# Two graph attention layers over 32 graphs: P.V of a unit in one block, and guard and shares of all twelve heads in one step

## Chip, cores and metric

The kernel runs on one core of a Trainium2 chip. The metric is the device time of one execution in microseconds (us), as the median of several. The engines are TensorE (PE; PEld is its weight load), VectorE (DVE), ScalarE (ACT), GpSimd (POOL) and SyncE (SP), which here only issues DMAs.

## The reference, cut to what matters

There are 32 graphs of 256 nodes with 384 features, an adjacency matrix of 256 x 256 for each, and 12 heads of 32.

```python
h = relu(layernorm(x))
x = x + L0(h, adj, adj)      # bias = adj + adj
h = relu(layernorm(x))
x = x + L1(h, adj)           # bias = adj

# one layer
q, k, v = heads(h @ Wq.T), heads(h @ Wk.T), heads(h @ Wv.T + bv)
a = q @ k.T * 384 ** -0.5 + bias          # per head, 256 x 256
a = where(any(a != 0, row), a, -inf)
out = nan_to_num(softmax(a)) @ v
return out @ Wo.T + bo
```

All of it is float32. The projections are computed with each operand split in a high and a low part and three products of the parts.

## The kernel before

A *unit* is one layer of one graph, so there are 64 units. Each engine runs its own program of *slots*: slot k works on four units at once, `attend` = k, `project` = k + 1, `output` = k - 1 and `norm` = k + 2. What an engine does in a slot, and in which order, is a list written out by hand, one list for each engine (`slot` and, for TensorE, `stages`). Nothing reorders it: an instruction that waits holds up everything behind it on its engine. Layer 1 of a graph comes three units after its layer 0, so its statistics need the result of unit k - 3.

The steps of a unit:

- **Rows.** VectorE takes statistics (L485) and the mean (L491), GpSimd computes `inv_dev` (`invert_deviation`, L296 and L298), VectorE the `shift` (L497), ScalarE `normalise` (L417), TensorE turns the rows (`transpose_rows`, L694), ScalarE copies the high part (`rows_high`, L425), VectorE makes the low part (`rows_low`, L504).
- **Projections.** `project_queries` and `project_keys` (L714) fill a PSUM bank for each third c of the features, 0, 1 and 2. ScalarE's `qk_high` (L435) and VectorE's `qk_low` (L512) take it out into `split_qk`, and SyncE's `stack_quadrant` (L242) copies the parts into `stack`, three DMAs for each of four quadrants. Each quadrant serves three heads. `qk_high` 0 waits until all stack DMAs of the unit before have landed, since they read `split_qk`. `project_v` (L733) and `add_value_bias` (L520) give `values`.
- **Scores.** For each head (a *step*, 0 to 11), `scores` (L640) makes a 256 x 256 tile in one of two banks, `negate_scores` (L535) adds the bias, negates and takes each row's minimum, and `exps` (L389) the exponential with its row sums.
- **Turning.** P.V needs the probabilities turned. Heads 0 to 3 are turned in 32 x 32 blocks on VectorE (`turn_blocks`, L549) and the blocks moved by 16 DMAs (`move_blocks`, L232); heads 4 to 11 go through TensorE (`transposes`, L652) and ScalarE (`copy_probT`, L401).
- **Guard.** GpSimd folds each tile in three additions (`add_half`, L308; `add_rest`, L313 and L318), so that VectorE's `find_share` can tell a row of zeros. It takes the reciprocals of the sums (L557), the largest magnitude (L559) and their product, the share (L562), once for each group of four heads.
- **P.V and shares.** `weigh_values` multiplies group 1 in one part (L660) and groups 0 and 2 in another (L669, L660). The shares are spread (`spread_shares`, L410), turned (`transpose_shares`, L746), copied (L444) and multiplied with the heads (`scale_heads`, L572). GpSimd splits the result (`split_heads`, L327 and L330), and `project_out` (L758) and `result` (L581) finish the unit.

Query, key, row, value and output products share two PSUM banks in turn. A stage that takes a bank waits for the reader of its last content:

```python
MISC = {"rows": (0, 1), "qk": (0, 1, 0), "out": (1, 1), "v": (0, 1)}
```

So query block 2 can start only when `qk_low` 0 has read bank 0. SyncE's list in a slot was: stack quadrants 2 and 3 of `attend`, loads, moves 1, 3 and 0, stack quadrants 0 and 1 of `project`, move 2, store. A move of `attend` waits for all four `turn_blocks` and for P.V of the unit before.

## Time and profile before

| | |
|---|---|
| median of three runs | 1602.06 us (1599.18 to 1602.61) |
| profiled execution | 1602.71 us |
| its span, first to last instruction | 1600.8 us |
| TensorE, weight load | 97%, 88% busy |
| VectorE, ScalarE, GpSimd | 86%, 86%, 82% busy |
| DMA engines | 71% busy, 163 GB/s |
| granted TensorE clock | 0.997 of full |

A line of the profile names the kernel's line (L714), the engine, and the tiles as output<-input. "Idle before" is the time in which an engine stood still in front of an instruction, with what ended it. Ends of matmuls are modelled and overlap their followers, so on TensorE distances from start to start are what counts. A merged row of a timeline (x16) gives the first start and the length to the last end.

### The profile page before, as it was taken

What the parts mean: (1) busy time and instruction counts of PE and PEld (TensorE: products, weight loads), DVE (VectorE), ACT (ScalarE), POOL (GpSimd) and SP (SyncE); (2) the same over time, 40 slices, a digit from 0 to 9 for tenths busy, and PEclk for the clock granted to TensorE, in tenths of its full rate; (3) what the DMA queues carried; (4) which work ended last, traced back from release to release, by engine and by line L of the source; (5) the groups of instructions that cost most, each with busy time, mean ns of one, the idle gap of its engine ahead of it and who ended that gap; (6) DMA issues with size and microseconds to landing.
All of it is one profiled execution on the core that took longest, in us unless ns stands there. A gap on an engine that the chain in (4) does not pass through costs nothing.

```text
span 1600.8 us, 45924 instructions
## 1 busy us (share of the span) xinstructions
PE 1550.4 (97%) x13184; PEld 1402.1 (88%) x13184; DVE 1372.1 (86%) x5190; ACT 1368.9 (86%) x4297; POOL 1320.1 (82%) x1673
## 2 busy tenths in 40 slices
PE   5999999999999999999999999999999999999996
PEld 5888998889889889888898899898898899898895
DVE  5898888888888888888888888888888888888895
ACT  5888888888889888888888888888888888888885
POOL 3788888888888888888888888888888888888885
PEclk9999999999999999999999999999999999999999
DMA  8677777676677676776776776766767767767664
GB/s 246 133 158 158 164 168 175 147 173 155 159 177 168 152 177 150 163 176 148 167 160 157 175 169 157 172 155 154 180 156 164 158 162 164 176 153 171 153 137 113
DMA packets 132538, 260.22 MB, mean 163 GB/s; under 512 B 30400, under 2 KB 58560, under 8 KB 132288
## 3 DMA queue, kind: packets, MB, share of 16 engines
q1 hardware_dynamic: 132288, 257.28, 70.4%
q8 instruction: 108, 1.77, 0.5%
q14 instruction: 142, 1.16, 0.2%
HBM read 26.48 MB, written 12.58 MB: 24 GB/s over the span
## 4 chain that ended last, share of the span: by engine, by line
PE 71%; SPq 14%; DMA 8%; DVE 2%; issue 2%; ACT 2%; POOL 0%; POOLq 0%; ACTq 0%; DVEq 0%
PE misc_bank L714 19%; PE misc_bank L758 12%; PE probT_bank L652 10%; PE misc_bank L733 10%; PE score_bank L640 8%; DMA stack<-split_qk 8%; SPq L242 7%; SPq L232 6%; PE values_bank L660 6%; PE values_bank L669 2%; PE misc_bank L694 2%; PE values_bank L746 2%; DVE split_qk L512 1%; ACT split_qk L435 1%; ACT prob L389 1%
## 5 line engine op out<-in xcount | busy, mean ns | idle before, releaser
L389 ACT ACTIVATE prob<-neg,guard 128x256 f32<-128x256 f32 x1536 | 764.2, 510 | 2.8 <-DVE guard L535 2.7
L308 POOL TENSOR_TENSOR half<-neg 128x256 f32<-128x256 f32 x768 | 550.9, 738 | 35.5 <-DVE guard L535 8.1
L535 DVE CUSTOM_DVE_ANT_0 neg<-score_bank,bias 128x256 f32<-128x256 f32 x1536 | 568.7, 416 | 7.6 <-PE score_bank L640 6.6
L401 ACT ACTIVATE probT<-probT_bank 128x512 f32<-128x512 f32 x512 | 290.8, 597 | 71.3 <-PE probT_bank L652 71.1
L640 PE MATMUL score_bank<-stack 96*128 96x256 f32 x1536 | 316.4, 308 | 2.9 <-DMA stack<-split_qk 1.7
L389 ACT ACTIVATION_READ_ACCUMULATOR prob<-neg,guard 128x1 f32 x1536 | 309.2, 201 | 0.0
L652 PE MATMUL probT_bank<-identity,prob 128*128 128x128 f32 x2048 | 307.3, 273 | 1.0 <-ACT prob L389 0.7
L313 POOL TENSOR_TENSOR half<-half 128x512 f32<-128x512 f32 x192 | 247.1, 1287 | 15.1
L640 PEld LDWEIGHTS score_bank<-stack 96*128 96x128 f32 x1536 | 221.1, 191 | 30.5 <-DVE guard L535 26.1
L652 PEld LDWEIGHTS probT_bank<-identity,prob 128*128 128x128 f32 x2048 | 242.4, 141 | 5.9 <-ACT prob L389 1.1
L435 ACT ACTIVATE split_qk<-misc_bank 128x512 fp32r<-128x512 f32 x192 | 114.6, 597 | 105.7 <-DMA stack<-split_qk 80.4
L512 DVE TENSOR_TENSOR split_qk<-misc_bank,split_qk 128x512 fp32r<-128x512 f32 x192 | 131.6, 685 | 79.0 <-ACT split_qk L435 79.0
L549 DVE STREAM_TRANSPOSE blocks<-prob 128x256 f32<-128x256 f32 x512 | 188.9, 416 | 1.6 <-ACT prob L389 1.1
L327 POOL TENSOR_SCALAR headsT_high<-headsT 128x256 fp32r<-128x256 f32 (+1 forms) x128 | 66.2, 517 | 107.9 <-DVE headsT L572 102.7
L318 POOL TENSOR_TENSOR guard<-half 128x256 f32<-128x256 f32 x192 | 141.5, 737 | 15.1
L520 DVE TENSOR_TENSOR values<-misc_bank,v_bias 128x384 f32<-128x384 f32 x128 | 71.0, 555 | 86.0 <-PE misc_bank L733 86.0
L330 POOL TENSOR_TENSOR headsT_low<-headsT,headsT_high 128x256 fp32r<-128x256 f32 (+1 forms) x128 | 130.4, 1019 | 10.7
L660 PE MATMUL values_bank<-probT,values 128*32 128x256 f32 x2048 | 135.5, 382 | 0.0
L341 POOL TENSOR_TENSOR rows<-rows,o_bias 128x384 f32<-128x384 f32 x128 | 127.0, 1013 | 0.0
L535 DVE DVE_READ_ACCUMULATOR2_ANT guard<- 128x1 f32 x1536 | 125.8, 82 | 0.0
L714 PE MATMUL misc_bank<-rowsT_high,w_low_0q 128*128 128x256 f32 x288 | 88.0, 305 | 14.6 <-DVE split_qk L512 10.7
L660 PEld LDWEIGHTS values_bank<-probT,values 128*32 128x32 f32 x2048 | 59.9, 109 | 43.8 <-issue 10.8
(92 smaller groups left out, 3988.3 us busy)
## 6 DMA issues: line engine op xcount, KB each, us to landing
stack<-split_qk SPq DMA_DIRECT2D x768, 192.0 KB, 3.7
moved<-blocks SPq DMA_DIRECT2D x1024, 64.0 KB, 2.0
rows<-x SPq DMA_DIRECT2D x32, 384.0 KB, 5.2
out<-rows SPq DMA_DIRECT2D x32, 384.0 KB, 2.8
bias<-adj SPq DMA_DIRECT2D x32, 256.0 KB, 5.2
neg<-w0q SPq DMA_DIRECT2D x1, 576.0 KB, 4.4
prob<-w0k SPq DMA_DIRECT2D x1, 576.0 KB, 6.4
probT<-w0v SPq DMA_DIRECT2D x1, 576.0 KB, 7.4
```

The costliest lines, as they stand in the source:

```text
L308: nc.gpsimd.tensor_tensor(half[:, step % GROUP, :, :], n[:, :, 0:N // 2], n[:, :, N // 2:N], ALU.add).then_inc(half_done, 1)
L313: nc.gpsimd.tensor_tensor(half[:, :, :, 0:N // 4], half[:, :, :, 0:N // 4], half[:, :, :, N // 4:N // 2], ALU.add).then_inc(quarter_done, 1)
L389: nc.scalar.activation(prob[:, step % PROB, q, :], neg[:, step % NEG, q, :], ACT.Exp, scale=-1.0, bias=guard[step // GROUP][:, step % GROU ...
L401: nc.scalar.activation(probT[:, n % PROBT, :, :].rearrange("p a b -> p (a b)"), probT_bank[n % 2][:, :], ACT.Copy).then_inc(act_copy_done, 1)
L535: nc.vector.tensor_tensor_reduce(out=neg[:, step % NEG, q, :], in0=score_bank[step % 2][:, q * N:(q + 1) * N], in1=bias[u.t % GRAPHS][:, q ...
L549: turn = nc.vector.transpose(blocks[:, :, :, at:at + HEAD], of)
L640: mm = nc.tensor.matmul(score_bank[step % 2][:, q * N:(q + 1) * N], stack[:, g, 0, c * N + q * P:c * N + (q + 1) * P], stack[:, g, 1, c * ...
L652: mm = nc.tensor.transpose(probT_bank[n % 2][:, k * N + q * P:k * N + (q + 1) * P], prob[:, step % PROB, q, k * P:(k + 1) * P], identity[: ...
L660: mm = nc.tensor.matmul(into[a * HEAD:(a + 1) * HEAD, :], values[u.k % 2][:, k, h * HEAD:(h + 1) * HEAD], probT[:, (h - MOVED) % PROBT, k, ...
L714: mm = nc.tensor.matmul(into, w[:, k, cols], r[:, k, :], start=(k == 0 and n == 0), stop=(k == CH - 1 and n == 2))
L733: mm = nc.tensor.matmul(misc_bank[MISC["v"][i]][:, 0:H], r[:, k, where], w[:, k, :], start=(k == 0 and n == 0), stop=(k == CH - 1 and n == 2))
L758: mm = nc.tensor.matmul(misc_bank[MISC["out"][i]][:, 0:H], r[:, k, where], w[:, k, :], start=(k == 0 and n == 0), stop=(k == CH - 1 and n ...
```

## The change

P.V of a unit becomes one block of 48 matmuls in the slot after its scores, and the two parts of the heads are now groups 0 and 1 (512 wide) and then group 2 (256 wide). `guard` becomes one tile for all groups, and `find_share` works once on all twelve heads. Row minima get two places, for even and odd units. The bias ring has three tiles, and a bias is loaded one slot later. All five lists are rewritten: among others all four stack quadrants of a unit are issued in one slot, in turn with the moves. The number of instructions on TensorE stays. The diff, cut to its core:

```diff
-        guard = [sb(f"guard{i}", [P, GROUP, TILES, 1 + N // 8]) for i in range(GROUPS)]
-        sums = [sb(f"sums{i}", [P, HEADS, TILES]) for i in range(2)]
+        guard = sb("guard", [P, GROUPS, TILES, GROUP, N // 8 + 2])
+        sums = [sb(f"sums{i}", [P, GROUPS, TILES, GROUP]) for i in range(2)]
...
-        NEG, PROB, PROBT = 4, 4, 8
+        NEG, PROB, PROBT = 4, 4, TURNED
...
-            return slice(0, GROUPS, 2) if part else slice(1, 2)
+            return slice(2, 3) if part else slice(0, 2)
...
-                sync.wait_ge(heads_ready, u.before(1).count(PARTS, 2))
+                sync.wait_ge(heads_ready, u.before(1).count(PARTS, 1))
...
+                    (load_rows, norm, 0), (load_bias, project, 0), (move_blocks, attend, 3),
+                    (move_blocks, attend, 2), (stack_quadrant, project, 0), (move_blocks, attend, 0),
+                    (stack_quadrant, project, 1), (move_blocks, attend, 1), (stack_quadrant, project, 2),
+                    (stack_quadrant, project, 3), (store, output, 0),
...
-                pool.wait_ge(guard_done, u.before(1).count(2 * GROUPS, 2 * g + 2))
-                nc.gpsimd.tensor_tensor(guard[g][:, :, :, 1:], half[:, :, :, 0:N // 8], half[:, :, :, N // 8:N // 4],
+                pool.wait_ge(guard_done, u.before(1).count(2, 2))
+                nc.gpsimd.tensor_tensor(guard[:, g, :, :, 1:1 + N // 8].rearrange("p q h a -> p h q a"), half[:, :, :, 0:N // 8], half[:, :, :, N // 8:N // 4],
...
-                groups, heads = part_groups(part), headsT[:, 0:1 + part, :]
+                groups, heads = part_groups(part), headsT[:, 0:2 - part, :]
...
+                    (split_heads, output, 1), (add_half, attend, 5), (add_half, attend, 6), (add_half, attend, 7),
+                    (add_rest, attend, 1), (add_half, attend, 8), (add_half, attend, 9), (invert_deviation, norm, 0),
+                    (add_half, attend, 10), (add_half, attend, 11), (add_rest, attend, 2), (add_half, project, 0),
+                    (add_half, project, 1), (add_output_bias, project, 0), (add_half, project, 2),
+                    (add_half, project, 3), (add_rest, project, 0), (split_heads, attend, 0), (add_half, project, 4),
...
-                act.wait_ge(heads_ready, u.count(PARTS, 0 if n >= GROUP else -1))
+                act.wait_ge(heads_ready, u.before(1).count(PARTS, 1 if step < 2 * GROUP else 2))
...
-                act.wait_ge(shares_done, u.count(GROUPS, 3 if part else 2))
+                act.wait_ge(shares_done, u.count(1, 1))
...
+                    (copy_probT, output, 7), (normalise, project, 0), (normalise, project, 1),
+                    (copy_probT, output, 8), (rows_high, project, 0), (rows_high, project, 1), (exps, output, 11),
+                    (copy_probT, output, 9), (exps, attend, 0), (exps, attend, 1), (spread_shares, output, 0),
+                    (exps, attend, 2), (copy_probT, output, 10), (copy_probT, output, 11), (copy_sharesT, output, 0),
+                    (spread_shares, output, 1), (exps, attend, 3), (qk_high, project, 0), (exps, attend, 4),
+                    (qk_high, project, 1), (copy_sharesT, output, 1), (exps, attend, 5), (exps, attend, 6),
+                    (copy_probT, attend, 4), (qk_high, project, 2), (exps, attend, 7), (copy_probT, attend, 5),
+                    (exps, attend, 8), (exps, attend, 9), (exps, attend, 10), (copy_probT, attend, 6),
...
+            def find_share(u, _):
+                dve.wait_ge(exp_done, u.count(2 * HEADS, 2 * HEADS))
+                nc.vector.reciprocal(inverse[:, :, :, :], sums[u.k % 2][:, :, :, :]).then_inc(guard_done, 1)
+                dve.wait_ge(eighth_done, u.count(GROUPS, GROUPS))
+                at = u.k % 2
+                nc.vector.tensor_reduce(largest[:, :, :, :].rearrange("p g q h -> p (g q h)"),
+                                        guard[:, :, :, :, at:at + 1 + N // 8].rearrange("p g q h a -> p (g q h) a"),
+                                        AX.X, ALU.max, apply_absolute_value=True).then_inc(guard_done, 1)
+                dve.wait_ge(guard_done, u.count(2, 2))
+
+                dve.wait_ge(spread_done, u.before(1).count(PARTS, PARTS))
+                nc.vector.scalar_tensor_tensor(out=share[:, :, :, :],
+                                               in0=largest[:, :, :, :], scalar=0.0, in1=inverse[:, :, :, :],
                                                op0=ALU.not_equal, op1=ALU.mult).then_inc(shares_done, 1)
...
+                    (qk_low, project, 0), (negate_scores, attend, 6), (scale_heads, output, 1), (qk_low, project, 1),
+                    (negate_scores, attend, 7), (negate_scores, attend, 8), (qk_low, project, 2),
+                    (result, output, 0), (negate_scores, attend, 9), (statistics, norm, 0),
+                    (negate_scores, attend, 10), (mean, norm, 0), (result, output, 1), (statistics, norm, 1),
+                    (mean, norm, 1), (negate_scores, attend, 11), (shift_rows, norm, 0),
+                    (add_value_bias, project, 0), (add_value_bias, project, 1), (negate_scores, project, 0),
+                    (rows_low, norm, 0), (rows_low, norm, 1), (negate_scores, project, 1), (find_share, attend, 0),
+                    (negate_scores, project, 2), (turn_blocks, project, 0), (negate_scores, project, 3),
+                    (turn_blocks, project, 1), (turn_blocks, project, 2), (negate_scores, project, 4),
+                    (scale_heads, attend, 0), (turn_blocks, project, 3), (negate_scores, project, 5),
...
-            def weigh_turned(u, g, into):
+            def weigh(u, g, into):
                 for k in range(TILES):
+                    of_blocks = moved[:, :, k, :].rearrange("p a (h q i) -> p h q a i", h=MOVED, q=TILES)
                     for a in range(GROUP):
                         h = GROUP * g + a
+                        of = of_blocks[:, h, :, :, :] if h < MOVED else probT[:, h - MOVED, k, :]
                         mm = nc.tensor.matmul(into[a * HEAD:(a + 1) * HEAD, :],
-                                              values[u.k % 2][:, k, h * HEAD:(h + 1) * HEAD],
-                                              probT[:, (h - MOVED) % PROBT, k, :], start=(k == 0), stop=(k == TILES - 1))
+                                              values[u.k % 2][:, k, h * HEAD:(h + 1) * HEAD], of,
+                                              start=(k == 0), stop=(k == TILES - 1))
                 return mm
 
+            def weigh_values(u, _):
+                pe.wait_ge(values_done, u.count(TILES, TILES))
+                for moves in blocks_moved:
+                    pe.wait_ge(moves, u.count(16 * QUADS, 16 * QUADS))
+                pe.wait_ge(act_copy_done, u.count(TURNED, 2 * GROUP - MOVED))
+
+                pe.wait_ge(heads_done, u.before(1).count(PARTS, 1))
+                weigh(u, 0, values_bank[0][:, 0:N])
+                weigh(u, 1, values_bank[0][:, N:2 * N]).then_inc(heads_ready, 1)
+                pe.wait_ge(act_copy_done, u.count(TURNED, TURNED))
+
+                pe.wait_ge(sharesT_done, u.count(PARTS, 1))
+                weigh(u, 2, values_bank[1][:, 0:N]).then_inc(heads_ready, 1)
...
-                pe.wait_ge(heads_done, u.count(PARTS, 1) if part else u.before(1).count(PARTS, 2))
-                for g in range(1 + part):
+                if part == 0:
+                    pe.wait_ge(heads_done, u.before(1).count(PARTS, 2))
+                else:
+                    pe.wait_ge(sharesT_done, u.count(PARTS, 1))
...
+                    (transpose_rows, project, 0), (transpose_rows, project, 1), (transposes, output, 9),
+                    (scores, attend, 1), (transposes, output, 10), (scores, attend, 2),
+                    (project_queries, project, 0), (transposes, output, 11), (scores, attend, 3),
+                    (project_keys, project, 0), (project_queries, project, 1), (scores, attend, 4),
+                    (transpose_shares, output, 0), (weigh_values, output, 0), (scores, attend, 5),
+                    (project_keys, project, 1), (scores, attend, 6), (transpose_shares, output, 1),
+                    (scores, attend, 7), (transposes, attend, 4), (project_queries, project, 2), (scores, attend, 8),
+                    (project_keys, project, 2), (scores, attend, 9), (project_out, output, 0),
+                    (transposes, attend, 5), (transposes, attend, 6), (scores, attend, 10), (project_out, output, 1),
+                    (scores, attend, 11), (project_v, project, 0), (transposes, attend, 7), (project_v, project, 1),
+                    (transposes, attend, 8), (scores, project, 0),
```

A line of "..." marks what is left out; the lists, `find_share` and `weigh_values` as they were stand in the code above. Other lines of the diff follow from these: `BIASES` for `GRAPHS` in the bias's index, `minimum(u)` (0 for even units, 33 for odd) where the row minimum is written and read, `2 - part` for `1 + part` in the widths of the shares.

## Rows read from the trace of the kernel before

**Rows 1.** The page's part 1: busy us, share of the span, instructions.

```profile
PE 1550.4 (97%) x13184; PEld 1402.1 (88%) x13184; DVE 1372.1 (86%) x5190; ACT 1368.9 (86%) x4297; POOL 1320.1 (82%) x1673
```

**Rows 2.** Timeline, TensorE: start us, length; the transposes that open four slots.

```profile
49.96 0.60 PE L652 MATMUL probT_bank<-identity,prob 128*128 128x128 f32 x4
...
782.87 0.60 PE L652 MATMUL probT_bank<-identity,prob 128*128 128x128 f32 x4
...
806.82 0.60 PE L652 MATMUL probT_bank<-identity,prob 128*128 128x128 f32 x4
...
1536.78 0.60 PE L652 MATMUL probT_bank<-identity,prob 128*128 128x128 f32 x4
```

**Rows 3.** The waits: us in total, times, longest us.

```profile
POOL headsT_high L327 <- DVE headsT L572: 102.7, 63, 3.1
POOL var_eps L296 <- DVE mean_var L491: 81.2, 64, 18.7
ACT split_qk L435 <- DMA stack<-split_qk: 80.4, 47, 3.0
...
PEld misc_bank L714 <- DVE split_qk L512: 22.7, 34, 1.6
...
PEld misc_bank L714 <- DVE rowsT_low L504: 19.3, 64, 1.6
```

**Rows 4.** Timelines of TensorE, VectorE, SyncE, ScalarE, 799 to 828 us.

```profile
799.82 0.60 PE L652 MATMUL probT_bank<-identity,prob 128*128 128x128 f32 x4
...
802.97 0.68 DVE L512 TENSOR_TENSOR split_qk<-misc_bank,split_qk 128x512 fp32r<-128x512 f32 x1
...
803.68 4.47 SPq L242 DMA_DIRECT2D stack<-split_qk  x6
808.25 3.27 SPq L232 DMA_DIRECT2D moved<-blocks  x4
...
812.24 5.10 SPq L242 DMA_DIRECT2D stack<-split_qk  x6
819.27 7.53 SPq L232 DMA_DIRECT2D moved<-blocks  x12
...
820.33 0.60 ACT L435 ACTIVATE split_qk<-misc_bank 128x512 fp32r<-128x512 f32 x1 [1.51 <-DMA stack<-split_qk]
```

**Rows 5.** Timeline, TensorE: the P.V blocks of one slot and what follows.

```profile
783.40 1.07 PE L660 MATMUL values_bank<-probT,values 128*32 128x256 f32 x16
784.40 0.45 PE L733 MATMUL misc_bank<-w_high_0v,rowsT_low 128*128 128x384 f32 x1
784.68 0.34 PE L733 MATMUL misc_bank<-w_low_0v,rowsT_high 128*128 128x384 f32 x1
...
792.00 1.07 PE L669 MATMUL values_bank<-moved,values 128*32 128x256 f32 x16
792.89 1.05 PE L660 MATMUL values_bank<-probT,values 128*32 128x256 f32 x16
```

**Rows 6.** Timelines of VectorE, GpSimd, TensorE, 781 to 790 us.

```profile
781.48 0.56 DVE L581 TENSOR_TENSOR rows<-misc_bank,rows 128x384 f32<-128x384 f32 x1
...
783.92 1.99 POOL L341 TENSOR_TENSOR rows<-rows,o_bias 128x384 f32<-128x384 f32 x2
...
783.99 0.96 DVE L497 SCALAR_TENSOR_TENSOR shift<-mean_var,inv_dev 128x2 f32<-128x2 f32 x1
...
787.30 0.49 PE L694 MATMUL misc_bank<-identity,normed 128*128 128x128 f32 x3
...
789.22 0.35 PE L714 MATMUL misc_bank<-rowsT_high,w_low_1q 128*128 128x256 f32 x1
```

**Rows 7.** The groups of instructions: count, busy us, mean ns, idle before.

```profile
L389 ACT ACTIVATE prob<-neg,guard 128x256 f32<-128x256 f32 x1536 | 764.2, 510 | 2.8 <-DVE guard L535 2.7
...
L308 POOL TENSOR_TENSOR half<-neg 128x256 f32<-128x256 f32 x768 | 550.9, 738 | 35.5 <-DVE guard L535 8.1 <-POOL guard L318 0.4
...
L559 DVE TENSOR_REDUCE largest<-guard 128x8 f32<-128x264 f32 x192 | 72.1, 376 | 1.3 <-POOL guard L318 1.3
```

124 lines of the change are left out of this document (28 added, 96 removed).

## Prediction

> **What bounds the kernel now.** I read the busy table first [rows 1]: TensorE is busy 1550.4 of 1600.8 us and the others at most 86%. So the time is TensorE's order of work plus whatever it waits for. Then I measured the slot. Its marker is the transpose block `(transposes, output, 8)`, which opens each slot of the old order. It stands at 49.96 us in the first full slot and at 1536.78 in the last, 61 slots later, with one ordinary slot at 782.87 to 806.82 [rows 2]. That is 1486.8 / 61 = 24.37 us per slot on average against 23.95 in the ordinary one. Reading all the slots off the same rows, about 25 of 61 are 23.94 to 23.99 long, none is shorter, and the longest are 25.6. So there is a firm floor of 23.94 and an irregular 0.43 above it.
>
> The waits name both [rows 3]. The irregular part is the weight load of L714 (`project_queries`, c = 2) waiting for `split_qk` of L512: it needs bank 0 back from `qk_low` 0. Behind that stands ScalarE's L435 (`qk_high` 0), which waits 80.4 us in 47 places for the DMAs of `stack`. TensorE stands up to 1.6 us there at a time. The regular part is L714 (c = 0) waiting 64 times, some 0.3 us each, for `rows_low`.
>
> The DMA chain behind the irregular part: `qk_low` 2 ends at 803.65, SyncE issues six stack DMAs, four moves, one store, six stack DMAs, and the last lands at 820.33, when ScalarE's `qk_high` 0 starts [rows 4]. That is 16.7 us; the last six stacks take 8.1 of it, from the first issue at 812.24 to the landing. SyncE's issue is most of a slot's length: 12 moves in 7.53 us are 0.63 each, six stacks in 4.47 are 0.75 each, so 16 and 12 of them are 19.1 us, before loads and stores.
>
> **The change part by part.** I lay one new slot out from t = 0 at `(transpose_rows, project, 0)`, with the block lengths of the old slot. TensorE gets the same instructions in another order: three transposes are 0.33 us, four 0.36 to 0.44, a score step 0.24 to 0.32, nine query or key matmuls 1.07, nine value or output ones 1.58, sixteen of P.V 0.89. With 0.39 of waiting before query block 0 that puts query 0 at t = 2.4, query 1 at 5.2, P.V at 7.0, query 2 at 12.2, its keys from 13.6 to 14.7, `project_out` at 14.9 and 17.6, `project_v` at 19.4 and 21.4, the next slot at 23.7. ScalarE, by its own order and lengths, comes to `qk_high` 0 at 9.2, to 1 at 11.4, to 2 at 14.7.
>
> *P.V in one block.* Sixteen P.V matmuls that stand alone take 1.00 us to the next kind (783.40 to 784.40) and leave the first matmul behind them at 0.28 where its fellows take 0.175 to 0.18; sixteen that are followed by more of their kind take 0.89 (792.00 to 792.89) [rows 5]. So one block end costs 0.11 + 0.10. The entry costs about as much again (0.33 from a score step where 0.23 is usual, and a first step 0.02 longer): 0.12. One of two ends and entries goes: 0.33 us a slot. Changes between transposes and other matmuls number the same in both orders (nine each), so they cost nothing. The block now waits for all moves and, before its last sixteen at 8.8, for the last `copy_probT`, done at 7.4; score step 5 and the keys are queued behind it. The moves land some 4 us before it. Nothing is added. TensorE's own work: 23.94 - 0.31 (the wait at L714, c = 0) - 0.33 = 23.30.
>
> *The wait for `rows_low`.* In the old order 1.92 us pass from `transpose_rows` 1 to L714 (787.30 to 789.22) over 1.6 us of work [rows 6]; in the new one the work in between is 1.67 (transposes 9 and 10, scores 1 and 2). `rows_high` 1 no longer stands behind `copy_probT` 9 on ScalarE, but `copy_probT` 8 and both `rows_high` come in one run. I keep 0.30. This gives a floor of 23.60.
>
> *The chain that feeds it.* `result` 1 at 781.48, statistics, mean, GpSimd's `inv_dev`, and `shift`, which ends at 784.95: 3.47 us [rows 6]. The shift of two numbers takes 0.96: it starts at 783.99, 0.07 behind GpSimd's L341, and ends when the first L341 does. In the new order an `add_half` (L308, 738 ns [rows 7]) follows `inv_dev` in place of L341, and one mean fewer stands in the chain (0.13). Then `normed` 1 comes 4.7 us after `project_out` 1, and TensorE reaches `transpose_rows` 1 at 4.84: no wait. If the shift kept its 0.96, 0.15 us a slot would come on top, 9 us in all.
> The Trainium skill (SBUF — State Buffer, "Who interferes with whom") has this as a rule: a VectorE instruction with two SBUF inputs waits for the whole of a GpSimd instruction that reads SBUF. The trace's 0.96 agrees. By the rule the merged `find_share` meets it once where three met it, but behind a longer GpSimd instruction (L341); this changes no term.
>
> *Guard and shares in one step.* Two of three reciprocals, reductions and share instructions go from VectorE. The reduction has 792 elements: between 0.38 (one old one, L559, 264 elements [rows 7]) and 3 x 0.38 = 1.13; I take 0.95, nearer the upper row, since its length grows with the elements. It starts after the last exponentials of the unit, at t = 2.9 by my layout, and its shares are done at about 4.7. The next `negate_scores` (step 2) ends at 5.4, and score step 4 needs it at 6.3: covered by 0.9. If the cover went, each 0.1 would cost 6 us. GpSimd must have its last `add_rest` ready by 3.0; it is ready at 1.7. The heads are now multiplied first 512 wide, then 256: `project_out` 0 at t = 14.9 waits for a GpSimd step of 1.2 us after a VectorE step that ends at 12.8: 0.9 spare.
>
> *Bias ring of three, load moved.* The load waits for a unit three back, which is past; it is 1.0 us of SyncE's time either way, and the bias is needed 10 us later. Nothing.
>
> *SyncE's order and the stall.* This is the large term. `qk_low` 2 took 3.8 us from the end of the key matmuls of c = 2 (799.82 to 803.65 [rows 4]); now it takes 1.5, since ScalarE reaches `qk_high` 2 just as they end. Behind it come 3 stacks, 4 moves, 3 stacks, 4 moves, 6 stacks: four moves more than now, the store behind instead of in between. Three stacks cost 1.9 us while the queue is not full and 2.25 at the pace of six (4.47); four moves cost 2.5 at the free pace and 3.27 behind six stacks. So the last six start between 8.8 and 11.0 us after `qk_low` 2, where now 8.6, and land 8.1 later. The queue never holds more than three stacks before them, so I take the free pace with a little more, 9.1: a chain of 17.2, with ends at 16.7 and 19.1. `qk_low` 2 ends at t = 16.2, so the last stack lands at 16.2 + 17.2 - 23.6 = 9.8. Query block 2 stands at t = 12.2 and wants `qk_low` 0 (in VectorE's order at 11.0 to 11.6), so the DMA may land as late as 10.5. There are 0.7 us of spare where there is none now. The chain has scattered by about 2 us from slot to slot (slots 23.94 to 25.6), so some slots still wait: 0.15 on average, and I add 0.10 for small margins (0.1 to 0.5 us) at `result` 0, `value_bias` 1 and ScalarE's `qk_high` 1. New slot: 23.60 + 0.25 = 23.85.
>
> *Head and tail.* The head has the same loads and waits: 0. At the end all shares of the last unit hang on its last exponentials, and two GpSimd splits (L327 and L330, 512 wide 2.0 and 256 wide 1.2 us) follow each other where one did: +2.4 us.
>
> **Sum.** 62 x (24.37 - 23.85) = 32.2; less 2.4: 29.8. Span 1600.8 - 29.8 = 1571.0. The profiled run took 1602.7, 1.9 over its span, and the median of the runs is 0.65 below it: 1571.0 + 1.9 - 0.65 = 1572.
>
> **Rivals.**
> (a) *SyncE becomes the bound; slower.* The last stack's landing releases `qk_high` 0, and on ScalarE stand between it and `qk_high` 2: one exponential step and two more after `qk_high` 1 (three steps of two instructions of L389 at 510 ns [rows 7], pipelined to 0.98 a step: 2.9 us), two `qk_high`, a shares copy, a probability copy; with `qk_low` 2 it is 6.1 us. That closes a loop with the DMA chain. At 17.2 it is 23.3, under the floor. At the upper end, 19.1, it is 25.2, and the slot is that long: 62 x 0.83 + 2.4 = +54, 1656. It decides from a chain of 18.3 on. For it: SyncE issues for 20 of 24 us now. Against: the queue drains while it issues moves.
> (b) *No change.* GpSimd has 1320 us of work, 21.3 a slot, and now waits 184 us, 3.0 a slot, in two places [rows 1, 3]. The new order has it wait for three results of others (both heads, the mean) with 2.3 us to spare at 23.6. If these waits stay at 3.0, the slot stays at 24.3: 1600.
> (c) *The spread is absorbed too.* Slot 23.60: 62 x 0.77 - 2.4 = 45: 1557. It rests on the landings: the last of the six stacks now lands 3.0 us after SyncE has issued it (817.34 to 820.33 [rows 4]).
> By the Trainium skill (DMA: Bandwidth & Descriptors, "Anatomy of one DMA", a fit for another issuing path) 192 KB would take 2.4 us, so the chain would be 0.6 shorter and the spare 1.3, which ends at (c); the 3.0 speak against it.
> (d) *The merging brings its block saving alone*, and the stall stays: 24.37 - 0.33 = 24.04, 1584.
>
> **Chances.** Forecast (1560 to 1580) 0.46; (d) 0.15; (c) 0.13; (b) 0.08; (a), whose price grows from nothing with the chain, 0.18. The range reaches from just under (c) to (b), 1553 to 1602, and leaves out (a). Within 0.2% (3.2 us, about what a measurement of this kernel can tell from no change) I put 0.08, which is (b); faster 0.74; slower 0.18.
>
> **What would show it.** Slot length 23.6 to 24.0; P.V as one run of 48 with 2.75 us; L714 waiting under 10 us for L512 and still about 19 for `rows_low`; L435 waiting for the stack DMAs under 40 us; one reduction per unit of 0.9 to 1.0 us; shift at 0.74. Wrong would be: L435 or L640 waiting for `stack` in nearly every slot (then (a)), GpSimd idle 3 us a slot (b), or TensorE waiting at `transpose_rows` or `project_out`.

## The result and the profile after

The changed kernel takes 1614.69 us (median of four runs, 1611.88 to 1618.81) where the kernel before takes 1601.69 on the same chip: a ratio of 1.0086, 95% interval 1.0061 to 1.011. It is slower. The forecast was 1572, and the range ended at 1602. The profiled execution has a span of 1610.1 us at a granted clock of 0.992.

The page's part 1 of the changed kernel (busy us, share of the span, instructions; compare [rows 1]) shows TensorE with 12 us less to do and VectorE with 18 us less, in a longer span:

```profile
PE 1538.4 (96%) x13184; PEld 1409.0 (88%) x13184; DVE 1353.7 (84%) x4806; ACT 1365.2 (85%) x4297; POOL 1322.6 (82%) x1673
```

The waits of the changed kernel, all engines (us in total, times, longest us), stand against [rows 3]:

```profile
ACT split_qk L439 <- DMA stack<-split_qk: 98.1, 57, 4.0
...
POOL var_eps L301 <- DVE mean_var L495: 59.9, 64, 17.8
...
PEld probT_bank L657 <- ACT prob L393: 48.1, 49, 2.3
...
PE probT_bank L657 <- ACT prob L393: 34.9, 42, 2.1
...
PEld misc_bank L709 <- DVE rowsT_low L508: 16.0, 64, 1.6
```

TensorE's wait at query block 2 is gone from this list. In its place `transposes` 4 (L657), which stands just ahead of query 2, waits for ScalarE's exponentials (L393). And ScalarE's `qk_high` 0 waits more for the stack DMAs than before: 98.1 us in 57 places against 80.4 in 47.

The timeline of TensorE gives the slots. The new slot opens with `transpose_rows` 0 (L689); here are the first full slot and the one 61 later (start us, length):

```profile
51.62 1.12 PE L689 MATMUL misc_bank<-identity,normed 128*128 128x128 f32 x6
...
1542.16 0.89 PE L689 MATMUL misc_bank<-identity,normed 128*128 128x128 f32 x6
```

That is 1490.5 / 61 = 24.43 us a slot, against 24.37 before [rows 2]. The shortest slots are 23.62 where they were 23.94. So the floor came down by the third of a microsecond that was forecast, and the irregular part above it rose from 0.43 to 0.81. The slots together are thus only some 4 us longer than before; the rest of the profiled 9.3 us is in the tail, which is 7.6 us longer, while the head is 2.5 shorter.

One ordinary slot shows how. From the timelines of VectorE, SyncE, ScalarE and TensorE of the changed kernel, 852 to 878 us (start us, length; idle before it in brackets):

```profile
852.79 0.69 DVE L516 TENSOR_TENSOR split_qk<-misc_bank,split_qk 128x512 fp32r<-128x512 f32 x1 [0.73 <-ACT split_qk L439]
...
853.51 1.83 SPq L247 DMA_DIRECT2D stack<-split_qk  x3
855.44 2.85 SPq L237 DMA_DIRECT2D moved<-blocks  x4
858.39 1.86 SPq L247 DMA_DIRECT2D stack<-split_qk  x3
860.35 2.86 SPq L237 DMA_DIRECT2D moved<-blocks  x4
863.31 4.77 SPq L247 DMA_DIRECT2D stack<-split_qk  x6
...
871.96 0.60 ACT L439 ACTIVATE split_qk<-misc_bank 128x512 fp32r<-128x512 f32 x1 [1.90 <-DMA stack<-split_qk]
872.46 0.50 ACT L393 ACTIVATE prob<-neg,guard 128x256 f32<-128x256 f32 x1
...
873.59 0.66 PE L657 MATMUL probT_bank<-identity,prob 128*128 128x128 f32 x4 [0.67 <-ACT prob L393]
...
876.45 0.40 PE L645 MATMUL score_bank<-stack 96*128 96x256 f32 x2
...
876.65 0.60 ACT L439 ACTIVATE split_qk<-misc_bank 128x512 fp32r<-128x512 f32 x1
...
877.28 0.69 DVE L516 TENSOR_TENSOR split_qk<-misc_bank,split_qk 128x512 fp32r<-128x512 f32 x1 [0.50 <-ACT split_qk L439]
```

`qk_low` 2 ends at 853.48, SyncE issues twelve stack DMAs with eight moves between them, the last one lands just before 871.96, `qk_high` 0 runs, exponential step 4 stands behind it on ScalarE, `transposes` 4 waits for that, then come query 2, keys 2, and the next `qk_low` 2, which ends at 877.97. This is a closed loop of 24.5 us, and it is the slot. On the average of 62 slots it is 18.24 (the DMA chain from the end of `qk_low` 2 to the last landing) + 1.73 (landing to `transposes` 4) + 2.88 (to the end of the keys, which is the start of the score step behind them, at 876.45 here) + 1.52 (to the end of `qk_low` 2) = 24.37.

### The profile page after: what moved, and what is told of

It reads as the page before. It is cut to its first block and busy times, and to the rows that moved or that the text cites. A ratio compares the mean times of both kernels' runs of the same rounds, so it can differ in the third digit from the quotient of the medians.

```text
span 1610.1 us, 45412 instructions
## 1 busy us (share of the span) xinstructions
PE 1538.4 (96%) x13184; PEld 1409.0 (88%) x13184; DVE 1353.7 (84%) x4806; ACT 1365.2 (85%) x4297; POOL 1322.6 (82%) x1673
## 5 line engine op out<-in xcount | busy, mean ns | idle before, releaser
L393 ACT ACTIVATE prob<-neg,guard 128x256 f32<-128x256 f32 x1536 | 762.2, 504 | 2.3 <-DVE guard L539 2.2
L313 POOL TENSOR_TENSOR half<-neg 128x256 f32<-128x256 f32 x768 | 556.5, 739 | 74.5 <-DVE guard L539 56.4
L645 PE MATMUL score_bank<-stack 96*128 96x256 f32 x1536 | 346.0, 308 | 6.2 <-DVE guard L539 4.8
L657 PE MATMUL probT_bank<-identity,prob 128*128 128x128 f32 x2048 | 299.7, 274 | 38.3 <-ACT prob L393 34.9
L393 ACT ACTIVATION_READ_ACCUMULATOR prob<-neg,guard 128x1 f32 x1536 | 300.7, 196 | 0.0
L657 PEld LDWEIGHTS probT_bank<-identity,prob 128*128 128x128 f32 x2048 | 240.2, 141 | 55.5 <-ACT prob L393 48.1
L645 PEld LDWEIGHTS score_bank<-stack 96*128 96x128 f32 x1536 | 238.1, 191 | 34.3 <-issue 25.5
L439 ACT ACTIVATE split_qk<-misc_bank 128x512 fp32r<-128x512 f32 x192 | 113.8, 593 | 118.4 <-DMA stack<-split_qk 98.1
L554 DVE STREAM_TRANSPOSE blocks<-prob 128x256 f32<-128x256 f32 x512 | 188.0, 412 | 2.1 <-issue 2.1
L332 POOL TENSOR_SCALAR headsT_high<-headsT 128x512 fp32r<-128x512 f32 (+1 forms) x128 | 66.0, 515 | 95.4 <-DVE headsT L578 92.7
L335 POOL TENSOR_TENSOR headsT_low<-headsT,headsT_high 128x512 fp32r<-128x512 f32 (+1 forms) x128 | 129.8, 1014 | 10.6
L346 POOL TENSOR_TENSOR rows<-rows,o_bias 128x384 f32<-128x384 f32 x128 | 127.2, 1014 | 0.0
L667 PE MATMUL values_bank<-probT,values 128*32 128x256 f32 x2048 | 123.3, 381 | 0.0
L587 DVE TENSOR_TENSOR rows<-misc_bank,rows 128x384 f32<-128x384 f32 x128 | 71.4, 558 | 55.5 <-PE misc_bank L756 55.5
L578 DVE TENSOR_TENSOR headsT<-values_bank,sharesT 128x512 f32<-128x512 f32 (+1 forms) x128 | 71.5, 558 | 47.5 <-PE values_bank L667 23.1
L667 PEld LDWEIGHTS values_bank<-probT,values 128*32 128x32 f32 x2048 | 67.0, 111 | 44.9 <-issue 1.7
```

What stands on the lines that cost most here:

```text
L313: nc.gpsimd.tensor_tensor(half[:, step % GROUP, :, :], n[:, :, 0:N // 2], n[:, :, N // 2:N], ALU.add).then_inc(half_done, 1)
L335: nc.gpsimd.tensor_tensor(headsT_low[:, groups, :], heads, headsT_high[:, groups, :].bitcast(F32), ALU.subtract).then_inc(heads_split_done, 1)
L393: nc.scalar.activation(prob[:, step % PROB, q, :], neg[:, step % NEG, q, :], ACT.Exp, scale=-1.0, bias=guard[:, step // GROUP, q, step % G ...
L554: turn = nc.vector.transpose(blocks[:, :, :, at:at + HEAD], of)
L645: mm = nc.tensor.matmul(score_bank[step % 2][:, q * N:(q + 1) * N], stack[:, g, 0, c * N + q * P:c * N + (q + 1) * P], stack[:, g, 1, c * ...
L657: mm = nc.tensor.transpose(probT_bank[n % 2][:, k * N + q * P:k * N + (q + 1) * P], prob[:, step % PROB, q, k * P:(k + 1) * P], identity[: ...
```

## Experiments

Theory A: that loop sets the slot, and the change's work on TensorE and VectorE is sound. Against it stood: SyncE or the DMA engines are simply full (the landing can't come earlier), the merged `find_share` is to blame, or the one P.V block is worth nothing. In the table, "exps 4 ahead" is exponential step 4 ahead of `qk_high` 0, and "turn 3" is `turn_blocks` 3 ahead of `scale_heads` 0. Landing is the mean time of the last stack DMA's landing, counted from the slot's start. Slots and landings come from one profiled execution of each kernel. The runs were made on several chips, on which the kernel before took 1601.2 to 1603.8 us; each ratio is to the kernel before on the same chip, so a difference between two medians of the table can be off by some 2 us. The *twin* of a run is the kernel that differs from it by the one edit in question.

| edit of the changed kernel | us | ratio to before, 95% | mean, shortest slot | landing |
|---|---|---|---|---|
| (kernel before) | 1602 | | 24.37, 23.94 | |
| none | 1614.7 | 1.0086 [1.0061, 1.011] | 24.43, 23.62 | 10.76 |
| exps 4 ahead | 1588.9 | 0.9914 [0.9882, 0.9946] | 24.01, 23.59 | 10.86 |
| move 1 ahead | 1641.2 | 1.0233 [1.0202, 1.0264] | 24.89, 23.99 | 10.57 |
| both | 1641.4 | 1.0236 [1.0213, 1.0259] | 24.87, 23.69 | 10.55 |
| find_share in three | 1627.7 | 1.0147 [1.0119, 1.0174] | 24.70, 23.86 | 10.97 |
| half of move 1 ahead | 1591.9 | 0.9936 [0.9913, 0.9959] | 24.14, 23.60 | 10.31 |
| exps 4, half move | 1579.6 | 0.9859 [0.9838, 0.988] | 23.90, 23.61 | 10.52 |
| four moves' DMAs left out | 1566.6 | 0.9775 [0.9755, 0.9796] | 23.71, 23.59 | 8.29 |
| P.V cut | 1614.0 | 1.0079 [1.0057, 1.01] | 24.57, 23.93 | 10.80 |
| exps 4, half move, P.V cut | 1587.9 | 0.9905 [0.9881, 0.993] | 24.08, 23.93 | 10.36 |
| exps 4, half move, turn 3 | 1567.6 | 0.9785 [0.9769, 0.9801] | 23.71, 23.59 | 9.81 |
| exps 4, half move, turn 3, find_share in three | 1605.7 | 1.0019 [1.0001, 1.0036] | 24.28, 24.17 | 10.14 |
| exps 4, half move, turn 3, tail filled | 1568.7 | 0.9784 [0.9766, 0.9802] | 23.74, 23.59 | 9.82 |

**Exponential step 4 ahead of `qk_high` 0 on ScalarE.**

```diff
-  (exps, attend, 3), (qk_high, project, 0), (exps, attend, 4),
+  (exps, attend, 3), (exps, attend, 4), (qk_high, project, 0),
```

> The changed kernel with one swap on ScalarE: (exps, attend, 4) ahead of (qk_high, project, 0). Theory A: transposes 4 waits because its exponentials stand behind qk_high 0, which waits for the last stack DMA; it starts 1.73 us after that landing, and the landing (10.8 us into the slot on average) is past the 10.1 that would be in time. With the swap only query block 2 depends on the landing, in time up to 10.7: the wait of transposes 4 goes from 0.69 us a slot to under 0.1, a wait of about 0.3 appears at query block 2, the mean slot goes from 24.43 to 23.95, the time from 1614.7 to about 1585. Theory B, that ScalarE as a whole is too full or the DMA chain bounds the slot wherever its result is read: time stays within 5 us of 1614.

1588.9 us, 25.8 less, where some 30 less was expected. The chain itself stays at 18.3, but the landing no longer holds `transposes` 4. The waits of this run show what is late next, the bank of query 2, as in the kernel before:

```profile
ACT split_qk L439 <- DMA stack<-split_qk: 50.1, 50, 2.4
PEld misc_bank L709 <- DVE split_qk L516: 18.6, 32, 1.6
...
PEld probT_bank L657 <- ACT prob L393: 3.2, 3, 1.5
```

One entry of a hand-written list turned the changed kernel from slower into faster than the one before.

The swap does more than free `transposes` 4, though. In the changed kernel ScalarE works without a gap from `qk_high` 0 to `qk_high` 2 (871.96 to 876.65 in the slot above; 0.03 us idle on average), so its own list reaches `qk_high` 2 at the same moment as TensorE's keys do. The swap shortens both ways (ScalarE now has 0.38 us idle in that stretch). No run shows which of the two would hold the loop alone.

**Move 1 ahead of the stack DMAs, alone and with the swap.** This was meant to shorten the chain, and it did the contrary.

```diff
-  (move_blocks, attend, 2), (stack_quadrant, project, 0), (move_blocks, attend, 0),
-  (stack_quadrant, project, 1), (move_blocks, attend, 1), (stack_quadrant, project, 2),
+  (move_blocks, attend, 2), (move_blocks, attend, 1), (stack_quadrant, project, 0),
+  (move_blocks, attend, 0), (stack_quadrant, project, 1), (stack_quadrant, project, 2),
```

> The changed kernel with one change in SyncE's list: move 1 goes ahead of stack quadrant 0, so only one group of four moves stands between qk_low 2 and the last stack DMA. Theory A: the four moves cost 2.95 us of issue in that chain while SyncE has 1.5 us of idle time ahead of it, so the landing comes 1.4 us earlier (9.3 us into the slot), transposes 4 waits under 0.1 us a slot, the mean slot is about 23.7 and the time about 1571. Rival C, that the chain is set by the DMA engines' throughput and not by SyncE's issue: the landing stays near 10.8 and the time near 1614.

> Both swaps together. Theory A: the landing is at 9.3 us and in time up to 10.7, so nearly no slot waits for it: slots of 23.62 to 23.7, about 1568 us, at most 4 us under the second swap alone. If each swap worked through a cause of its own, the gains would add up to some 70 us.

Both missed by some 70 us. VectorE's and SyncE's timelines of the first of them show the reason:

```profile
784.88 0.76 DVE L554 STREAM_TRANSPOSE blocks<-prob 128x256 f32<-128x256 f32 x2
...
785.71 7.94 SPq L237 DMA_DIRECT2D moved<-blocks  x12
793.74 1.86 SPq L247 DMA_DIRECT2D stack<-split_qk  x3
795.70 2.85 SPq L237 DMA_DIRECT2D moved<-blocks  x4
798.64 7.83 SPq L247 DMA_DIRECT2D stack<-split_qk  x9
```

The moves can't start before `turn_blocks` 3 (L554) ends at 785.64, and twelve of them take 7.94 us. Stack 0 starts 2.3 us later than `qk_low` 2 allows (it ends at 791.47), and score steps 0 and 3 of the next unit, the first readers of quadrants 0 and 1, now wait for their stacks (`PEld score_bank L645 <- DMA stack<-split_qk` rises from 3.5 us to 77.6). I had counted SyncE's wait in front of stack 0 as room, and not measured it: 75.5 us in 53 places, 1.4 us each, is room for two DMAs, not for four.

**Half of move 1 ahead.** Two of its four DMAs go ahead of stack 0, two stay:

```diff
+  def move_half(u, part):   # the DMAs 2 * part and 2 * part + 1 of move 1
...
+  (move_blocks, attend, 2), (move_half, attend, 0), (stack_quadrant, project, 0), (move_blocks, attend, 0),
+  (stack_quadrant, project, 1), (move_half, attend, 1), (stack_quadrant, project, 2),
```

> The changed kernel with the first two of the four DMAs of move 1 issued ahead of stack 0, the other two where the whole move stood. Theory A (the loop of landing and qk_high sets the slot): the chain from qk_low 2 to the last landing is 18.24 us in the changed kernel, of which two issues of a move are 1.45, and SyncE idles 1.4 us a slot in front of stack 0. The chain falls to 16.8, the loop of 24.37 to 22.9, under the floor of 23.62: slots of 23.75, 1573 us; ScalarE's qk_high waits for the DMAs about 20 us in all instead of 98. Theory B (SyncE is bound by the release of the buffer of moves, as it was with the whole of move 1 ahead): stack 0 starts later by what was put ahead of it, the last landing stays at 10.8 and the slot at 24.4: 1615. Theory C (DMA bandwidth sets the landing): as B.

> The same half of move 1 ahead of stack 0, and exponential step 4 ahead of qk_high 0 on ScalarE as in the run that had this alone (1588.9, slots of 24.01). Theory A: nothing waits for the DMAs any more; slots of 23.68, the time 1588.9 - 61 x 0.33 = 1569 us. Theory B or C: 1589, as without the half move.

The direction was right and the size half of what was expected: 22.8 us instead of 42 alone, and 9.3 instead of 20 on top of the swap. Stack 0 now starts 0.7 us later in the slot on average, since the ten moves ahead of it are not always done when `qk_low` 2 is, and of the 1.45 us only 0.45 reached the landing (10.76 to 10.31).

**The chain made shorter for certain.** Two DMAs of move 0 and two of move 1 are left out for every unit but the first (half of the quadrants 0 and 1 of P keeps old values, so this leaves work out):

```diff
-                for of in range(QUADS):
+                for of in range(QUADS if u.k == 0 or to > 1 else 2):
```

> The changed kernel with only two of the four DMAs of move 0 and of move 1 issued, for every unit but the first: half of the quadrants 0 and 1 of P keeps the values of the first unit, so part of the computation is left out. Nothing else is moved. Theory A: the chain is four issues shorter, 18.24 - 2.9 = 15.3 us, the loop is 21.5, and only the floor of 23.62 is left: slots of 23.65, 1614.7 - 61 x 0.79 = 1567 us. If the slots stayed above 23.9, something other than SyncE's chain would hold them.

1566.6 us, where 1567 was expected. So close a match is partly luck, since the slots fall to 23.71 for 23.65 and the chain to 15.8 for 15.3. No compute engine's work is changed, only what SyncE issues between the stacks. The wait of `qk_high` 0 for the DMAs is all but gone:

```profile
ACT split_qk L441 <- DMA stack<-split_qk: 4.2, 2, 4.0
```

What this run can't tell is whether the issues or the bytes count, since with four DMAs of 64 KB less, less data moves too. Nor does any other run. From the start of stack 0 to the last landing it is 18.1 us in the changed kernel, and each move less in that stretch takes 0.55 to 0.62 us off it (two fewer in the half moves, four fewer here and with all of move 1 ahead), less than the 0.74 from one move's issue to the next. The last six stacks of the changed kernel are issued 0.75 us apart but land 1.09 apart. They take 8.1 to 8.3 us from first issue to last landing in every version that issues them as a run of six. And the DMA engines are not far from full over the chain (length; PE, PEld, DVE, ACT and POOL busy us; granted clock; DMA share; GB/s; changed kernel, the slot above):

```profile
855.40:863.30 7.90, 7.86 (x57) 7.61 (x56) 6.74 (x23) 7.17 (x24) 6.63 (x10) 1.00 0.83 177
863.30:872.00 8.70, 8.70 (x98) 7.26 (x99) 8.33 (x32) 6.80 (x24) 7.47 (x10) 1.00 0.88 200
```

So it is shown that the chain through SyncE's queue sets the slot, and that it can be made shorter; how much of its pace is SyncE's issue and how much the transfers' stays open. The next run leaves nothing out.

**Turn the blocks earlier.** If SyncE's start hangs on `turn_blocks` 3, the cure is on VectorE, where `scale_heads` 0 stands ahead of it:

```diff
-  (scale_heads, attend, 0), (turn_blocks, project, 3), (negate_scores, project, 5),
+  (turn_blocks, project, 3), (scale_heads, attend, 0), (negate_scores, project, 5),
```

> Exponential step 4 ahead of qk_high 0, half of move 1 ahead of stack 0 (1579.6 us, slots of 23.90), and now also VectorE's turn_blocks 3 ahead of scale_heads 0. In the run without this, SyncE's first move starts at t = 10.6, 0.12 us after turn_blocks 3 ends, and ten moves are issued before stack 0, which starts 1.0 us after qk_low 2 has ended. Theory A (the chain from turn_blocks 3 through the moves to the last landing): everything on SyncE comes up to 0.7 us earlier, stack 0 at the end of qk_low 2; the last landing at 9.8 instead of 10.5; slots of 23.70 and 1579.6 - 61 x 0.20 = 1567 us. Rival: the heads are scaled 0.8 us later, GpSimd's split with them, and project_out 0 starts to wait at t = 14.9, or the release of `moved` by P.V (matmul 32 at t = 8.8) is the later of the two: 1580 or slower.

1567.6 us, where 1567 was expected; all the work is done, and this version takes 2.1% less than the kernel before (interval 2.0 to 2.3%) and 2.9% less than the changed kernel, by its median on another chip. VectorE's and SyncE's timelines of it:

```profile
820.53 0.84 DVE L561 STREAM_TRANSPOSE blocks<-prob 128x256 f32<-128x256 f32 x2
821.29 0.65 DVE L585 TENSOR_TENSOR headsT<-values_bank,sharesT 128x512 f32<-128x512 f32 x1
...
821.45 5.40 SPq L237 DMA_DIRECT2D moved<-blocks  x8
826.95 1.17 SPq L244 DMA_DIRECT2D moved<-blocks  x2
828.21 1.86 SPq L254 DMA_DIRECT2D stack<-split_qk  x3
830.17 2.83 SPq L237 DMA_DIRECT2D moved<-blocks  x4
```

SyncE starts 0.08 us after the turning, 0.83 us earlier in the slot than without the edit (9.76 against 10.59), the landing comes at 9.8, and `qk_high` 0 waits 7.8 us in all. GpSimd and `project_out` 0 have their spare time for the later heads. It also shows that `moved`, which P.V has to release, is not the later of the two conditions: the matmul that releases it ends at about 8.9, and the turning at 9.61.

**P.V cut in two again.** 32 matmuls, score step 5, 16 matmuls:

```diff
-  (transpose_shares, output, 0), (weigh_values, output, 0), (scores, attend, 5),
+  (transpose_shares, output, 0), (weigh_values, output, 0), (scores, attend, 5), (weigh_values, output, 1),
```

> As the run before with exponential step 4 and half of move 1 ahead, and with P.V cut in two again: 32 matmuls, score step 5, 16 matmuls, in the same slot. It prices the one block. My working had 0.33 us a slot for one end and one entry of a P.V block: where nothing but TensorE's own work bounds the slot, 61 x 0.33 = 20 us above its uncut twin, some 1589 us. If the one block is worth nothing on the path, the two are within 4 us of each other.

> The changed kernel with P.V cut in two again (32 matmuls, score step 5, 16 matmuls), nothing else. The cut costs TensorE 0.32 us a slot, in front of the place at which it waits for the landing (transposes 4, 0.69 us on average). Theory A: the loop through SyncE does not contain P.V, so the cost is taken out of the wait: 41 of 62 slots wait longer than 0.33 us, and what is left over the others is 0.09 a slot, 5 us: 1620 us, the shortest slot 23.94, the wait down to 0.45. If P.V were on the path in every slot: 1634.

With the DMA wait mostly out of the way, the shortest slot goes from 23.61 to 23.93: the block end and entry cost 0.32 us, where I had 0.33. The time rises by 8.3 us only, since in slots that still wait somewhere the wait shrinks instead. In the changed kernel itself the cut costs nothing in the medians (1614.0 against 1614.7), where 1620 was expected; the profiled execution was the slowest of its four (1619.8 us), and its slots are 0.14 longer. The floor rises by 0.31 and the wait at `transposes` 4 falls from 0.69 to 0.49. So the change's best part, 0.32 us a slot of the floor, was real and was eaten by the loop. It would be 20 us in all if nothing else held any slot; no run shows it whole.

**find_share in three group steps**, at the place of the one:

```diff
+  for g in range(GROUPS):
+      nc.vector.reciprocal(inverse[:, g, :, :], sums[u.k % 2][:, g, :, :]).then_inc(guard_done, 1)
...
-  act.wait_ge(shares_done, u.count(1, 1))
+  act.wait_ge(shares_done, u.count(GROUPS, GROUPS))
```

> The changed kernel with find_share in three steps, one per group of four heads, at the same place in VectorE's list: three reciprocals, reductions and share instructions in place of one of each, some 1.0 us more of VectorE a slot. Theory A: the step after it is needed 0.9 us later than it ends and the slot waits for DMAs anyway, so the time moves by less than 5 us (1612 to 1620). If the merged step carried the kernel's gain or its loss, it would move by 10 us or more (64 us for each us that is not covered).

> The run with turn_blocks 3 ahead (1567.6 us, slots of 23.71, 0.1 above the floor), with find_share back in three group steps at its new place. The three steps take VectorE 3 x (0.48 + 0.37 + 0.19) = 3.1 us a slot against 0.74 + 0.92 + 0.30 = 2.0 for the one; in the changed kernel the same edit made ScalarE wait 0.76 us a slot for the last share and TensorE 0.2 us around score step 4, and turn_blocks 3 ended 0.55 later. Theory A (both places count): 0.2 from score step 4 and 0.1 from a landing 0.55 later than now: slots of 24.0, 1586 us. Rival (only SyncE's chain feels it, as in the loop of the changed kernel): slots of 23.8, 1574. Rival (three steps at this place are hidden where SyncE has slack): within 3 us of the twin.

It costs 13 us in the changed kernel by the medians (10 by the two ratios, which is 1.0147 against 1.0086) and 38 in the best one, so I had twice taken it too lightly. The groups of the first of these runs:

```profile
L569 DVE SCALAR_TENSOR_TENSOR share<-largest,inverse 128x8 f32<-128x8 f32 x192 | 92.5, 482 | 6.6
L563 DVE TENSOR_REDUCE largest<-guard 128x8 f32<-128x264 f32 x192 | 71.6, 373 | 0.0
L561 DVE RECIPROCAL inverse<-sums 128x8 f32<-128x8 f32 x192 | 37.1, 193 | 2.9 <-ACT prob L393 2.9
```

and of the changed kernel:

```profile
L562 DVE TENSOR_REDUCE largest<-guard 128x24 f32<-128x792 f32 x64 | 58.9, 920 | 0.2 <-POOL guard L323 0.2
L568 DVE SCALAR_TENSOR_TENSOR share<-largest,inverse 128x24 f32<-128x24 f32 x64 | 47.1, 736 | 2.2
L559 DVE RECIPROCAL inverse<-sums 128x24 f32<-128x24 f32 x64 | 19.1, 298 | 2.9 <-ACT prob L393 2.9
```

3 x 1.05 = 3.1 us a slot against 1.95. In the kernel before, with the three steps spread over the slot, the same instructions took 3 x 0.87 = 2.6, since a share instruction took 0.31 us there and not 0.48. ScalarE waits 0.76 us a slot for the last share, and in the best kernel the shortest slot is 24.17. There the waits add a place that I hadn't named:

```profile
DVE headsT L586 <- POOL headsT_low L342: 19.8, 57, 2.3
```

`turn_blocks` 3 ends 0.8 us later than in the twin (10.44 against 9.61), and `scale_heads` 0 behind it and GpSimd's split are later too. VectorE's second `scale_heads` waits for that split. `negate_scores` 7 and 8 are queued behind it on VectorE, which TensorE feels after keys 2 (0.30 us a slot) besides the 0.21 around score step 4.

**The tail filled.** In the last unit, 36 transposes of the identity, computed for nothing, stand in front of `project_out` 0:

```diff
+                if u.k == UNITS - 1 and i == 0:
+                    for _ in range(36):
+                        nc.tensor.transpose(misc_bank[0][:, 0:P], identity[:, :], identity[:, :])
```

> The run with turn_blocks 3 ahead, and in the last unit 36 transposes of the identity into a bank that is free (computed for nothing) between the last shares' transposes and project_out 0, where TensorE has nothing to do for 3.6 us while the heads are split. It asks whether the half clock in the tail comes of that idleness. If it does: both project_out blocks of the last unit take 1.6 us instead of 2.7 and 3.3, 2.8 us less than its twin. If the clock falls all the same, the two are within 1 us, or up to 1 us slower where the filling overruns.

1568.7 against 1567.6 us, no difference that could be told. Two stretches of each profile (length; PE, PEld, DVE, ACT and POOL busy us; granted clock; DMA share; GB/s). Without filling:

```profile
1556.00:1559.00 3.00, 2.37 (x9) 1.86 (x8) 0.56 (x1) 0.00 (x0) 0.00 (x0) 0.61 0.00 0
1559.00:1562.00 3.00, 2.98 (x9) 2.74 (x9) 0.00 (x0) 0.00 (x0) 0.00 (x0) 0.50 0.02 5
```

and with it:

```profile
1553.00:1556.00 3.00, 3.00 (x34) 1.38 (x28) 0.69 (x1) 0.00 (x0) 0.14 (x1) 0.50 0.00 0
...
1559.00:1562.00 3.00, 3.00 (x25) 3.00 (x24) 0.00 (x0) 0.00 (x0) 0.70 (x1) 1.00 0.00 0
```

In the filled kernel both `project_out` blocks ran at the full clock, and from the last shares' transposes to the end it took 11.95 us (1556.45 to 1568.4) where the twin took 14.05 (1551.75 to 1565.8). But ahead of that its P.V block had run at half clock, 5.2 us instead of 2.7, so nothing was left of it. In each of the two profiles the clock was low for a part of the tail, only in another place. In the filled kernel it was low (0.74) already from 1540 to 1545 us, ahead of the filling. One profile of each doesn't settle what makes it fall; that stays open.

## Why the prediction was wrong, step by step

The profiled span came out 39.1 us above the forecast of 1571.0, and the median 3.3 us further from the span than I had put it. Of the 39.1, the slots are 61 x (24.43 - 23.85) = 35.7, the tail 5.2 and the head -2.5; the sum had also counted 62 gains for 61 slots, 0.5. What failed is the stall at the stack DMAs, which I had put at 0.15 us a slot with a spare of 0.7: the chain was 1.0 us longer than my term for it, and the deadline 0.4 us earlier.

**The floor: right.** 23.62 for 23.60. P.V's one block is 2.73 us for 2.75, cutting it costs 0.32 for 0.33. The wait for `rows_low` was 0.25 for 0.30 (16.0 us in 64 places), `qk_low` 2 ends 1.52 us after the keys for 1.5. The reduction takes 0.92 us for 0.95. No wait appeared at `transpose_rows` or `project_out`.

**The chain: the failed step, in its size.** I had 17.2 us, "the free pace with a little more", and it was 18.24. The small term is what SyncE needs ahead of the last six stacks: they start 10.1 us after `qk_low` 2 instead of 9.1, and land 8.1 later, as I had it (averages of 61 slots). Four moves take 2.9 us to issue, twice, where I used the 2.5 of twelve moves in a row (7.53 / 3 [rows 4]). The rows that were to hand gave both ends of the range, 2.5 and 3.27 for four moves, and the mean of them was the truth. (The lower end of my range for the chain, 16.7, doesn't follow from its own terms either: 8.8 + 8.1 is 16.9.)

**The deadline: the failed step, in its kind.** I asked when query block 2 needs `qk_low` 0 and got 10.5. But ScalarE's own list has exponential step 4 behind `qk_high` 0, and TensorE's has `transposes` 4 ahead of query 2: that path is 1.73 us long and ends at 11.83, so the landing has to come at 10.1. The waits show it: none of TensorE at query block 2 for `qk_low` 0, and 48.1 us of the weight load at `transposes` 4. The layout had both times in it, and I followed one of the two users of the late instruction. With a landing at 10.76 on average and a deadline of 10.1, 42 slots wait, 0.69 us on average over all, where I had 0.15.

**Rival (a)** is what happened: a loop of the DMA chain and 6.1 us, and its sign too (`qk_high` 0 waits for the stack DMAs in 57 of 64 units). Its 6.1 us were added up along ScalarE's own list; the same 6.13 were measured along TensorE's, and the two end together, as said above. The chain measured 18.24 and the loop 24.37, which is the slot of the kernel before to the hundredth, and that is chance: by rival (a) alone the change would have been worth nothing, and slower only from a chain of 18.3 on. That the kernel is slower than before comes more from its tail. I gave the rival 0.18. What should have raised that is its threshold, only 1.1 us above my own figure for a chain of twenty issues, each known to about a tenth. Nearer still, its loop passes the floor of 23.60 from a chain of 17.5 on, 0.3 above my figure, and from there on the forecast has no spare. Rivals (c) and (d) are out by the times. The sign that I had named for (b) did show, GpSimd idle 3 us a slot: its waits are 92.7, 59.9 and 56.4 us, 3.4 a slot in all. But it isn't what holds the slots. TensorE waits for GpSimd only in the first and the last unit (3.8 us in 2 places), and with `turn_blocks` 3 ahead the slots fell to 23.71 with nothing changed on GpSimd, whose waits fell to 2.8 a slot. The sign was badly chosen, since an engine off the path waits as long as the slot is.

**`find_share`: right in the changed kernel, wrong in the reason.** The cover of 0.9 us that I named is what the merged form has: three steps are 1.2 us longer, and 0.2 of that came through to TensorE around score step 4. The three old steps at this place would have cost 10 to 13 us. The share instruction costs more than its work: of 24 numbers it takes 0.73 to 0.75 us in 63 units, in which GpSimd's L346 starts 0.3 us ahead of it and ends 0.04 ahead of its end, but 0.18 in the last unit, where GpSimd has nothing to do. By the Trainium skill (SBUF — State Buffer, "Who interferes with whom") VectorE and GpSimd hold a shared port pair in turns. The two durations agree with it, and so does the `shift` (0.97 before, 0.71 now, with a shorter GpSimd instruction behind `inv_dev`). The three share instructions of the group steps took 0.48 each at this place, and 0.31 each at their old ones, so what they cost depends on where they stand.

**The tail: half right.** From the opening of the last slot (`transpose_rows` 0 at 1542.16 us, before at 1540.43) to the end it is 67.9 us against 60.3. The chain of waits of the changed kernel, last stretch (start us, length, what):

```profile
1588.45 0.99 DVE largest L562
...
1590.37 0.66 PE values_bank L744 x4
1591.02 3.53 PE values_bank L667 x32
...
1594.58 0.70 DVE headsT L578
...
1596.13 1.27 POOL headsT_low L335
...
1597.53 0.44 DVE headsT L578
...
1599.40 3.23 PE misc_bank L756 x9
...
1603.28 3.26 PE misc_bank L756 x9
```

and of the kernel before:

```profile
1588.83 0.70 DVE headsT L572
...
1591.72 2.99 PE misc_bank L758 x9
...
1595.34 1.88 PE misc_bank L758 x9
```

From the last unit's first multiplication of heads on this chain to `project_out` 0 it is 4.82 us (1594.58 to 1599.40) against 2.89 (1588.83 to 1591.72): that is the second GpSimd split, 1.9 us for my 2.4. What I didn't have is the granted clock. It was at half (1.2 of 2.4 GHz) for most of P.V's first 32 matmuls, 3.53 us where 1.9 is usual, and for both output blocks, 6.49 us where before, with only the first at half clock, they took 4.87: 3.2 us together. The remaining 2.4 us lie ahead of P.V. The chain there runs through GpSimd's last folds, `find_share` (1588.45) and the shares' transposes (1590.37), behind which P.V stands in the new list; before, it ran through ScalarE's copies of the probabilities. No run prices that.

## What to carry to other kernels

A late event has as many deadlines as it has users: follow every instruction queued behind the waiting one on its engine, and every engine that reads their results, and take the earliest deadline. Where a wait ends in a DMA chain that starts from the engine it holds up, add up the whole loop and compare it with the floor; the margin between them, and not the mean of a spare, tells how safe a gain elsewhere is. And idle time in front of an issue is room only for as many issues as fit into it, counted from the event that really starts the queue.

## What the runs showed of the hardware

The pace at which SyncE issues DMAs depends on the mixture: 64 KB moves cost 0.66 us each in a run of twelve (7.94 us), 0.72 in a group of four between stacks (2.85 to 2.86), and six or nine stack DMAs of 192 KB cost 0.76 to 0.87 each, three alone 0.62. Two groups of four are 0.7 us more than the 2.5 each that I had read off a run of twelve, as much as the whole spare that I had counted on. The DMA engines were 83 to 88% busy over the chain of the slot shown, and the last six stack DMAs landed 1.09 us apart though they were issued 0.75 apart, so the pace may be set by the transfers as much as by the issue; that is open.

A VectorE instruction of 24 numbers with two inputs took 0.18 us with GpSimd idle and 0.74 beside it, when it ended with GpSimd's instruction; cutting it into three made it 3 x 0.48. Small instructions with two inputs are dear beside a busy GpSimd, and in this kernel their number and their place counted more than their size.
